# Square roots of two batches in a row, bodies written out, and each score product issued twice

## The reference

```python
q2 = jnp.sum(Q * Q, axis=-1, keepdims=True)
k2 = jnp.sum(K * K, axis=-1, keepdims=True)
sq = q2 + jnp.swapaxes(k2, -1, -2) - 2.0 * jnp.einsum('bhqd,bhkd->bhqk', Q, K)
dist = jnp.sqrt(jnp.maximum(sq, 0.0))
W = (SHEP_EPS + dist) ** (-SHEP_P)
W = W / (SHEP_EPS + jnp.sum(W, axis=-1, keepdims=True))
A = jnp.einsum('bhqk,bhkd->bhqd', W, V)
O = (G * A).transpose(0, 2, 1, 3).reshape(b, t, d)
return X + jnp.einsum('btd,ed->bte', O, W_out) + b_out
```

## Time and profile before

| | |
|---|---|
| median of 3 runs | 1515.87 us (1515.39 to 1519.79) |
| profiled execution | 1515.65 us |
| its span in the trace | 1513.9 us |
| attention: first score product | 816.4 us after the span's start |
| attention: end of the last exponentials | 1221.4 us |
| busy over the span | PE 86%, DVE 84%, ACT 73%, POOL 59% |
| granted clock of TensorE, mean of the span | 0.899 |

### The profile page before, as it was taken

How to read it: one execution, slowest core, us unless ns; L and a number is a source line. 1 busy time by engine, 2 the same in 40 slices (tenths; PEclk the granted TensorE clock), 3 DMA queues, 4 the chain that set the end, 5 groups by cost and what they waited for, 6 DMA issues and landing times. The chain is left out here.

```text
span 1513.9 us, 21515 instructions
## 1 busy us (share of the span) xinstructions
PE 1302.8 (86%) x6448; PEld 636.5 (42%) x6448; DVE 1271.4 (84%) x2150; ACT 1098.4 (73%) x1594; POOL 900.4 (59%) x1054
## 2 busy tenths in 40 slices
PE   4788888998997599999997787788888579999998
PEld 3344445544553244444442233333333234444443
DVE  3999999999999988888886888888878568888885
ACT  4677877786777456556653899999999956656564
POOL 5999889989988666665665232322222026656655
PEclk8999999999999999999998677867666689999999
DMA  7122113111311043322220000000000023333331
GB/s 252 57 73 95 56 56 102 65 56 56 111 56 57 10 166 144 131 112 112 112 112 0 1 1 0 0 0 0 0 0 1 1 113 120 120 119 119 146 155 61
DMA packets 27923, 111.54 MB, mean 74 GB/s; under 512 B 4049, under 2 KB 9570, under 8 KB 19426
## 3 DMA queue, kind: packets, MB, share of 16 engines
q1 hardware_dynamic: 27010, 110.21, 19.4%
q10 hardware_dynamic: 864, 0.74, 0.2%
HBM read 108.06 MB, written 2.88 MB: 73 GB/s over the span
## 5 line engine op out<-in xcount | busy, mean ns | idle before, releaser
L1042 POOL TENSOR_TENSOR e_h_lo<-e_h,e_h_hi 128x512 f16<-128x512 f32 x272 | 314.7, 1158 | 246.4 <-ACT e_h_hi L1124 233.6
L275 POOL TENSOR_TENSOR m_h<-m_b_sb,m_dx 128x512 f32<-128x512 f32 x256 | 347.0, 1383 | 45.6 <-POOLq L67 35.8
L690 DVE TENSOR_TENSOR_SCAN m_h<-m_decay,m_h 128x1024 f32<-128x1024 f32 x112 | 255.9, 2285 | 10.9 <-DVEq L60 7.5
L393 PE MATMUL m_y_ps<-m_hc,ident 128*128 128x512 f32 x512 | 251.1, 614 | 0.0
L528 ACT ACTIVATE m_decay<-m_delta,mw_a_log 128x255 f32<-128x255 f32 x448 | 185.1, 461 | 87.7 <-DVEq L695 87.5
L1119 ACT ACTIVATE e_g<-e_g 128x512 f32<-128x512 f32 x256 | 148.9, 582 | 122.7 <-PE e_g L1064 121.5
L1124 ACT ACTIVATE e_h_hi<-e_h 128x512 f16<-128x512 f32 x272 | 169.7, 624 | 84.6 <-DVE e_h L1175 82.9
L1621 DVE TENSOR_SCALAR a_d<-a_s 128x512 f32<-128x512 f32 x256 | 170.3, 687 | 54.9 <-PE a_s L1508 35.9
L1064 PE MATMUL e_g<-ef_x_hi,ew_gate_up 128*128 128x512 f16 x544 | 207.3, 381 | 4.7 <-PEq L103 3.2
L1069 PE MATMUL e_y<-e_h_hi,ew_down 128*128 128x512 f16 x544 | 205.9, 379 | 2.1 <-POOL e_h_lo L1042 2.1
L1064 PE MATMUL e_u<-ef_x_hi,ew_gate_up 128*128 128x512 f16 x544 | 207.4, 381 | 0.0
(11 more groups left out here) (236 smaller groups left out, 2080.4 us busy)
## 6 DMA issues: line engine op xcount, KB each, us to landing
e_c_rest<-mix SPq DMA_DIRECT2D x48, 1024.0 KB, 8.7
m_b_sb<-b_rows SPq DMA_DIRECT2D x64, 512.0 KB, 5.4
ef_c_head<-mix SPq DMA_DIRECT2D x16, 1024.0 KB, 4.6
ew_gate_up<-w_gate_up SPq DMA_DIRECT2D x1, 2176.0 KB, 13.9
out<-x_sb SPq DMA_DIRECT2D x8, 256.0 KB, 2.3
ew_down<-w_down SPq DMA_DIRECT2D x1, 1088.0 KB, 11.1
mw_conv_rows<-w_conv_rows ACTq DMA_DIRECT2D x1, 640.0 KB
mix<-ef_cT SPq DMA_DIRECT2D x16, 32.0 KB, 1.6
```

The costliest lines, as they stand in the source:

```text
L275: ins = nc.gpsimd.tensor_tensor(h[:, m % 4, :, c], b_sb[:, p, 2 * m:2 * m + 2], dx[:, p, c:c + 1].to_broadcast([P, 2, T]), ALU.mult)
L393: ins = nc.tensor.matmul(y_ps[:], ident[:], hc[:, m % 2, n].rearrange("p c t -> p (c t)"), start=(m == 0 and n == 0), stop=(m == PAIRS - 1 ...
L690: nc.vector.tensor_tensor_scan(flat, decay_of(m, p)[:], flat, 0.0, ALU.mult, ALU.add).then_inc(scan_chain, 1)
L1042: nc.gpsimd.tensor_tensor(h_lo[:, k], h[:, k], h_hi[:, k], ALU.subtract).then_inc(h_lo_ready, 1)
```

## The change

Three things, all in the attention layer.

1. `d` and `gate` get a third buffer, and the heads run two batches ahead instead of one: body b holds the heads of batch b + 2, and the preparation of batch b + 3. ScalarE takes the square roots of batches 1 and 2, then 3 and 4, up to 13 and 14, together: in an odd body the roots of batch b and b + 1 come first, then the other table is loaded, then logarithms and exponentials of b; in the even body that follows only logarithms and exponentials. Batches 0 and 15 are done alone. v still has two buffers, and a new semaphore `v_free` lets POOL keep the next v when the last sums are read (h = 2).
2. There is no loop: 18 bodies, -2 to 15, are written out. In body -2 (`opening`) the preparation of batch 1 comes behind the 16 heads (all of it at h = 15) instead of between them.
3. `score` issues its two products, and then the same two again, into the same bank.

```diff
+        BUFS, LEAD = 3, 2
-        gate = sb("gate", [P, 2, TT, W])
-        d = sb("d", [P, 2, NH, TT * T])
+        gate = sb("gate", [P, BUFS, TT, W])
+        d = sb("d", [P, BUFS, NH, TT * T])
...
-            prologue()
-            body(-1, 1, core=False, tail=False)
-            body(0, 0, tail=False)
-            with eng.Fori(0, NB // 2 - 2) as i:
-                body(i * 2 + 1, 1)
-                body(i * 2 + 2, 0)
-            body(NB - 3, 1, further=False)
-            body(NB - 2, 0, further=False, ahead=False)
-            body(NB - 1, 1, further=False, ahead=False, heads=False, last=True)
+            def run(b):
+                body(b, b % 2, b % BUFS, b % 2 == 1, opening=b == -LEAD, core=b >= 0, tail=b >= 1, keeps=-1 <= b < NB - 1,
+                     heads=b < NB - LEAD, ahead=b < NB - LEAD - 1, further=b < NB - LEAD - 2, single=b in (0, NB - 1), last=b == NB - 1)
+
+            for n in range(-LEAD, NB):
+                run(n)
...
-                for kc in range(TT):
+                for kc in (*range(TT), *range(TT)):
                     ins = nc.tensor.matmul(s_ps[h % 2][:, kc * T:(kc + 1) * T], qkT[rows, p, 1, g, kc * P:(kc + 1) * P], qkT[rows, p, 0, g, :], start=True, stop=True)
...
-                    if h == 1 and ahead:
-                        front.transpose_z(pe, t_ps[0])
-                    if h == 8 and ahead:
+                    if h == (15 if opening else 1) and ahead:
+                        front.transpose_z(pe, t_ps[0])
+                    if h == (15 if opening else 8) and ahead:
                         front.project(pe, t_ps)
...
-                for first, n in ((0, 8), (8, 4), (12, 4)):
-                    take(act, d_ready)
-                    nc.scalar.activation(heads_of(first, n), heads_of(first, n), ACT.Sqrt).then_inc(act_chain, 1)
-                nc.scalar.preload_act_table_set("natural_log_exp_and_others")
+                def root(buffer):
+                    for first, n in ((0, 8), (8, 4), (12, 4)):
+                        take(act, d_ready)
+                        nc.scalar.activation(heads_of(buffer, first, n), heads_of(buffer, first, n), ACT.Sqrt).then_inc(root_chain, 1)
+                if single or paired:
+                    root(k)
+                    if not single:
+                        root((k + 1) % BUFS)
+                    act.wait_ge(root_chain, 3 if single else 6)
+                    act.sem_inc(root_chain, -3 if single else -6)
+                    nc.scalar.preload_act_table_set("natural_log_exp_and_others")
...
+                if b >= 2:
+                    take(pool, gate_free)
                 if tail:
-                    take(pool, gate_free)
-                if heads:
-                    keep(1 - p)
+                    take(pool, v_free)
+                if keeps:
+                    keep(1 - p, (k + 1) % BUFS)
...
-                    if h == 0 and ahead:
-                        front.normalise(dve, b + 2)
+                    if h == (15 if opening else 0) and ahead:
+                        front.normalise(dve, b + LEAD + 1)
...
                     if h == 2 and tail:
                         read_av(0)
-                    if h == 2 and tail:
                         read_av(1)
-                    if h == 4 and ahead:
+                        dve.sem_inc(v_free, 1)
+                    if h == (15 if opening else 4) and ahead:
                         front.read_zT(dve, t_ps[0])
```

More of the change, by code:

```diff
@@ L1473, in _, with keep, body @@
         def _(pool):
-            def keep(p):
+            def keep(p, k):
                 nc.gpsimd.tensor_scalar(v[:, p, :, :, 0:DH], front.by_head(p, 2), 1.0, 1.0, ALU.mult, ALU.mult).then_inc(v_ready, 1)
[L1477 to L1482, removed]
+                nc.gpsimd.tensor_scalar(gate[:, k], qkvg[:, p, :, 3 * W:4 * W], 1.0, 1.0, ALU.mult, ALU.mult).then_inc(gate_ready, 1)
+            def body(b, p, k, paired, opening, core, tail, keeps, heads, ahead, further, single, last):
                 if last:
                     experts.norm(pool)
+                if opening:
+                    front.norm(pool)
                 if ahead:
-                    front.residual(pool, b + 2)
+                    front.residual(pool, b + LEAD + 1)
+                if b >= 2:
+                    take(pool, gate_free)
                 if tail:
-                    take(pool, gate_free)
-                if heads:
-                    keep(1 - p)
+                    take(pool, v_free)
+                if keeps:
+                    keep(1 - p, (k + 1) % BUFS)
                 if ahead:
-                    front.pack(pool, p)
+                    front.pack(pool, 1 - p)
                 if further:
                     front.norm(pool)
-            batches(pool, body, prologue, lambda: None)
+                if last:
+                    take(pool, gate_free)
+            batches(pool, body, lambda: None)
         @block.tensor
@@ L1538, in project_out, with body @@
                 ins.then_inc(y_ready, 1)
-            def body(b, p, core=True, tail=True, heads=True, ahead=True, further=True, last=False):
+            def body(b, p, k, paired, opening, core, tail, keeps, heads, ahead, further, single, last):
                 for h in range(NH):
@@ L1572, in body @@
                             weights.wait(g, not tail)
-                            weigh(g, p)
+                            weigh(g, p, k)
                 if heads:
-                    scores_read.end(not core, False)
+                    scores_read.end(opening, False)
                 if core:
-                    weights.end(not tail, not heads)
+                    weights.end(not tail, last)
             def epilogue():
                 weights.wait(HG - 1)
-                weigh(HG - 1, 1)
+                weigh(HG - 1, (NB - 1) % 2, (NB - 1) % BUFS)
                 transpose_av()
@@ L1657, in update, with body @@
                 nc.vector.tensor_tensor(own, u_ps[:, 512:512 + TT * DM].rearrange("p (a d) -> p a d", a=TT), own, ALU.add)
-            def body(b, p, core=True, tail=True, heads=True, ahead=True, further=True, last=False):
+            def body(b, p, k, paired, opening, core, tail, keeps, heads, ahead, further, single, last):
                 for h in range(NH):
                     if heads:
-                        distance(h, 1 - p)
-                    if h == 0 and ahead:
-                        front.normalise(dve, b + 2)
+                        distance(h, (k + LEAD) % BUFS)
+                    if h == (15 if opening else 0) and ahead:
+                        front.normalise(dve, b + LEAD + 1)
                     if last:
@@ L1698, in body @@
                     if h == 15 and ahead:
-                        front.read_qkT(dve, p, t_ps)
+                        front.read_qkT(dve, 1 - p, t_ps)
                 if heads:
```

57 lines of the change are left out of this document (28 added, 29 removed).

## The result

The changed kernel takes 1561.38 us, the median of 4 runs (1559.8 to 1563.11), against 1517.25 (1515.39 to 1519.79) for the kernel before: a ratio of 1.0284 [1.0272, 1.0297]. It is 2.8% slower. The profiled execution is 1562.54 us, its span 1560.8.

The account below looks back on a forecast made before the run. ScalarE bounds the kernel, with TensorE and VectorE only 0.5 us a batch behind. 13.9 us lost at the start and 15.4 won back take 1515.65 to 1514.2 us; own range 1510 to 1519, 8 in 10 from 1507 to 1526.

Parts of the forecast that it names:

- Does the clock rise?: Attention stage: 512 more score products fill TensorE's gaps, so most of the stage is then at 2.4 GHz.
- T = 23.0: One body of TensorE and VectorE after the change, in us: 23.87 before, lower bound 22.8.
- Rival 2: TensorE and VectorE become the bound, since the clock rises only in part: time 1523 to 1535, chance 0.24.
- T = 25.0: Upper bound in us for one body of TensorE and VectorE, clock as now; time 1535.
- exposed heads: Heads where VectorE has no other work to cover doubled products: head 0 (0.24), head 2 (about 0.17), head 5 (0.25 becomes 0.33).
- The rest is hidden: Other heads' doubled products are covered by VectorE's copies, gating and splitting; without cover 3.8 us in a body.
- The margin: How far TensorE and VectorE's own pace stands behind ScalarE's 24.353 us a batch: only 0.5 us in a batch.
- The opening: Start of the attention layer, to the end of batch 2's exponentials: the lead of two batches costs 13.9 us, bounds 9 and 16.
- 18 loads of 1.28 us: ScalarE: 32 table loads become 18, saving 18.0 us and nothing more than the load; a pair takes 46.14 us.
- Written-out bodies at nothing: Attention layer's bodies written out instead of looped: priced at nothing, bounded by 0.1 us a body either way.
- A second product whose weight load is hidden: Doubled score products: a second product adds 0.12 or 0.19 us, without waiting for its weight load of 0.094.
- rival 3: Doubled products wait for their weight loads, 0.094 us each, at three exposed heads: time 1519.7, chance 0.05.

Follow-up runs that it names:

- e2: Kernel before with only the score products issued twice: 1551.36 us, ratio 1.0211.
- e8: Kernel before with two extra score products a head over 128 rows, ahead of the real ones: 1528.85 us, ratio 1.0086.
- e10: Changed kernel with products doubled only for heads 13, 14, 15, 0, 1 and 2: 1545.41 us, ratio 1.0182.
- e7: Changed kernel with products doubled only for heads 3 to 12: 1533.43 us, ratio 1.01.
- e1: Changed kernel with each score product issued once: 1525.6 us, ratio 1.0052.
- e3: Changed kernel with the two extra products of a head over 128 rows instead of 32, ahead of the real ones: 1553.24 us, ratio 1.023.
- e9: e5 with two extra products a head over 128 rows, at heads 3 to 12 only: 1529.38 us, ratio 1.008.
- e11: e9 with its extra products only from body 1 on, and eight more such products behind head 9: 1541.9 us, ratio 1.0156.
- e4: Kernel before with only the attention layer's loop over 12 bodies written out: 1520.03 us, ratio 1.0016.
- e5: e1 with the preparation of batch 1 put back between the heads of batch 0: 1523.44 us, ratio 1.0028.
- e12: e5 with each batch's roots by themselves again, 32 table loads, heads still two batches ahead: 1518.93 us, ratio 1.0011.

## Why the prediction was wrong

**The step that failed** is "Does the clock rise?", where I wrote that "512 more score products fill just these gaps. I take it that most of the stage is then at 2.4 GHz". They filled the gaps and the clock stayed: 0.68, and 0.66 in e2, where the doubling is the only edit. From that followed T = 23.0 for one body of TensorE and VectorE, and with it a sum in which ScalarE paces. Rival 2, to which I gave 0.24, is what happened, and more: its T of 25.0 "with the clock wholly as now" is 315.3 / 12 = 26.3 in the trace. e8 and e2 differ only in the extra products, which cover 128 rows in one and 32 in the other, so the premise that a busy TensorE means a fast clock is what was wrong. The rows that I read spoke against it already: TensorE was busy 8.36 of 9.39 us at 0.50 and 5.39 of 7.90 at 1.00. The Trainium skill, "TensorE: Matmul & The Clock Gate", Part 1, says that the clock gate follows how busy the array has been of late, and gives idle as the state of the lower level. The trace disagrees as far as busy is read from the profile: 0.50 with 15.23 of 16.00 us busy.

**T = 25.0 as the upper bound was too low**, by the list of exposed heads. I had head 0, head 2 and head 5. In the trace of the changed kernel head 2 does not wait after the opening, head 9 waits up to 0.70 where it had 0.27, and in the longest body heads 14, 15 and 0 wait 0.65, 1.46 and 1.77: TensorE's row from 940.38 on is one chain without a gap, in which score products alternate with weighted sums and transposes at 1.9 each, and each group of four adds 0.43 (1.03 against 0.60). e10 confirms that such heads cost: 14.8 / 12 = 1.2 us a batch for six. "The rest is hidden" holds nearly by itself (e7, 0.3 to 1.5 us in 12 batches) but not with the others: about 1 us a batch appears only with both. I read this as the same in-order chain, in which the middle heads' spare time is what let the late ones catch up; that the clock lies elsewhere in the body (0.76 against 0.69 and 0.68) is the other reading, and no run parts them.

**The margin was overrated even without the doubling.** e1 keeps 24.0 us a batch where I needed 23.1. I had read that "bodies at 22.97 and 23.35" were near what the faster clock gives, and 23.87 is where the stage stays. What T is with the clock wholly at the higher level and all heads doubled, e3 shows: 23.35, for the 23.0 of my sum. Its 128-row products make VectorE wait 0.88 at head 0 and 0.24 at head 2, where the changed kernel's make it wait 0.78 and not at all; less these 0.34, an estimate for 32 rows is 23.0. So the term was right, and its condition was not met. (The bodies of 22.68 in e9 and e11 have no extra products at heads 13 to 2 and are another case.)

**The opening was mis-sized, 20.8 us for 13.9, beyond my bound of 16.** From the first distance, by my own terms: batch 0's heads 14.3 for 13.9, the preparation 16.3 for 15.0, body -1 23.9 for 21.6, batch 2's heads 21.4 for 18.7, ScalarE 32.6 for 32.4, together 6.9. Most of it, 5.0, lies in the two bodies of doubled products, which I had priced at a clock that rises and then, from body 0 on, at the higher one; it was 0.57 and 0.66. The doubling makes 7.3 of the 20.8: batch 0's heads run from 820.0 to 834.3, 2.8 longer than e1's, the preparation 0.7, the rest 3.8. That e1, without the doubling, comes to 13.5 is no confirmation of 13.9, which was for doubled products: the two agree by luck.

**Right or nearly so.** 18 loads of 1.28 us, with nothing beside the load: a pair is 46.14 us plus its waits, to 0.1 in 315.3 (0.4 in e1's 287.9). Written-out bodies at nothing: right for the attention layer (e4). A second product whose weight load is hidden: four take 0.61 at the higher clock, where my sum had 0.63 (1.03 for 0.98 at the lower), and rival 3 is not needed. For example (e2):

```profile
992.92 0.60 PE L1508 MATMUL a_s<-af_qkT 32*128 32x256 f16 x4
```

**The sum by measured terms:** opening 108.5 for 101.6 (+6.9), batches 3 to 14 315.3 for 276.8 (+38.5), the start 820.0 for 817.0 (+3.0): 48.4 of the 48.3 between 1562.54 and 1514.2.

**Still open:** what besides the rows of a product decides the clock, so that the same code has 0.69 in e1 and 0.76 in e5; the 12.3 us that come only when all heads are doubled; why e8 and e11 spread; and what moves the start of the layer by up to 4.6 us from profile to profile.

## What to carry to other kernels

Before an engine's work is cut, ask what the next one keeps with its own clock as it is now, and take a faster clock into a sum only where a run shows it: here 15.4 us of table loads met a second bound 0.5 us behind, and won 4.3 (5.5 in e5). Filler for a clock is work in an in-order queue; price it at the slow clock and over the longest stretch without a gap, not at the places that wait today. And joining two batches to share a fixed cost makes the first pair wait for its second batch, once: 9.1 us here, against 15.4 of loads and 6.6 that the pairs gave back between e12 and e5.

## What the runs showed of the hardware

- Products of 32 rows hold the clock far less than products of 128 rows with as many columns: 0.66 (e2) against 0.91 (e8) over the same stretch of the same schedule, with products of neighbouring heads side by side in the first and not in the second.
- TensorE can be at its lower level while its row in the trace has no gap: 0.50 over 10.20 us busy of 10.20 in e9, right after a wait of 1.42. In the changed kernel it stays there over 16.00 us with 15.23 of them busy.
- An extra pair of score products adds 0.22 us at the higher level (0.61 for four, 0.39 for two) and 0.43 at the lower (1.03 and 0.60). Two heads that follow one another without a wait, each with its own 32 rows, overlap: the eight products from 937.01 on take 1.04 at the lower level, as long as the four of one head (1.03). With four of the eight over 128 rows they do not: 2.2 at the lower level (e9, 1020.88 to 1023.07).
